# An output projection in twelve rounded products in a token-mixing and mixture-of-experts kernel

## The reference, cut to what matters

```python
x_prev = concatenate([zeros_like(x[:, :1]), x[:, :-1]], axis=1)
xk, xv, xr = (x_prev + (x - x_prev) * tm for tm in (tmk, tmv, tmr))
k, v, r = xk @ Wk.T + bk, xv @ Wv.T + bv, xr @ Wr.T + br
wkv = _wkv_scan(k, v, time_decay, time_first)   # a recurrence over time
out = (sigmoid(r) * wkv) @ Wo.T + bo            # the output projection
x1 = layernorm(x + out)
# each token goes to the best of 8 experts: probs = softmax(x1 @ wg)
y = layernorm(x1 + gate * (x1 @ W[expert].T + b[expert]))
```

## Time and profile before

| | |
|---|---|
| median of 3 runs | 608.55 us (607.44 to 608.61) |
| the profiled execution | 608.08 us, span 606.4 us |
| TensorE busy | 566.6 us (93%) |
| VectorE busy | 530.0 us (87%) |
| ScalarE busy | 436.2 us (72%) |
| GpSimd busy | 281.4 us (46%) |
| mean granted clock of TensorE | 0.978 of full speed |

### The profile page before, as it was taken

The page is one execution under the profiler, slowest core; times in us unless marked ns, Lnnn a source line. Parts: engine busy times, 40 slices in busy tenths (PEclk is TensorE's granted clock), DMA queues, the critical chain, the costliest instruction groups (busy, mean ns, idle before and its releaser), DMA issues. The chain is left out here.

```text
span 606.4 us, 8730 instructions
## 1 busy us (share of the span) xinstructions
PE 566.6 (93%) x2404; PEld 408.3 (67%) x2404; DVE 530.0 (87%) x815; ACT 436.2 (72%) x838; POOL 281.4 (46%) x221
## 2 busy tenths in 40 slices
PE   4997689999999999999999999999989999999990
PEld 1444466677677768767776866885557888788880
DVE  6889989998998999899899989899999698766760
ACT  3637656677587667758766775956975998899982
POOL 2768515544452553445355344531051565666631
PEclk9999799999999999999999999999997999999996
DMA  9352550094046109305701920767854696878840
GB/s 348 138 70 81 203 66 0 1 248 101 0 174 139 36 14 247 85 0 187 141 17 39 251 57 1 221 138 265 256 162 134 184 255 205 266 228 224 237 150 0
DMA packets 40984, 84.46 MB, mean 139 GB/s; under 512 B 8751, under 2 KB 8751, under 8 KB 40818
## 3 DMA queue, kind: packets, MB, share of 16 engines
q1 hardware_dynamic: 30482, 56.67, 28.4%
q0 software_dynamic: 10464, 27.33, 20.9%
HBM read 66.95 MB, written 35.65 MB: 169 GB/s over the span
## 5 line engine op out<-in xcount | busy, mean ns | idle before, releaser
L1168 POOL TENSOR_TENSOR mixed<-unsplit,mixed 128x1024 fp32r<-128x1024 f32 x42 | 100.0, 2402 | 117.9 <-ACT mixed L775 117.9
L705 PE MATMUL y_ps<-w_e_hi,xgT 128*128 x312 | 108.8, 410 | 0.4 <-issue 0.4
L539 PE MATMUL y_ps<-w_o,rw 128*128 128x512 f32 x224 | 100.8, 594 | 0.0
L526 PE MATMUL vb<-mixed,w_kvr 128*128 128x512 f32 x336 | 87.8, 411 | 6.9 <-DVE evn L1375 6.8
L526 PE MATMUL kb<-mixed,w_kvr 128*128 128x512 f32 x336 | 82.4, 394 | 5.7 <-POOL mixed L1168 3.1
L526 PE MATMUL rb<-mixed,w_kvr 128*128 128x512 f32 x336 | 86.8, 407 | 0.9 <-DVE ee L1389 0.9
L526 PEld LDWEIGHTS vb<-mixed,w_kvr 128*128 128x128 f32 x336 | 63.4, 193 | 24.9 <-DVE evn L1375 8.9
L526 PEld LDWEIGHTS kb<-mixed,w_kvr 128*128 128x128 f32 x336 | 62.1, 188 | 21.6 <-DVE state L1343 5.2
L526 PEld LDWEIGHTS rb<-mixed,w_kvr 128*128 128x128 f32 x336 | 62.5, 188 | 19.5 <-issue 5.7
L1184 POOL TENSOR_TENSOR ee<-ee,state 128x512 f32<-128x512 f32 x32 | 35.0, 1092 | 86.8 <-DVE state L1359 86.1
L1326 DVE SCALAR_TENSOR_TENSOR unsplit<-diff,vec,xb 128x512 f32<-128x512 f32 x96 | 68.2, 772 | 5.3 <-PE kb L526 5.0
(11 more groups left out here) (233 smaller groups left out, 1105.7 us busy)
## 6 DMA issues: line engine op xcount, KB each, us to landing
bias<-b_experts SPq DMA_DIRECT2D x39, 256.0 KB, 4.6
x_biased<-bo POOLq DMA_DIRECT2D x8, 1024.0 KB, 17.4
w_e_raw<-w_experts SPq DMA_DIRECT2D x8, 1024.0 KB, 7.9
rows<-x_biased SPq DMA_DIRECT2D x28, 256.0 KB, 3.5
x_rows<-rows SPq DMA_DIRECT2D x28, 256.0 KB, 6.7
xb<-xT SPq DMA_DIRECT2D x4, 1026.0 KB, 5.4
xb<-xT SPq DMA_DIRECT2D x3, 1024.0 KB, 5.1
w_raw<-w_square SPq DMA_DIRECT2D x2, 1024.0 KB, 10.4
```

The costliest lines, as they stand in the source:

```text
L526: mm = pe.matmul(bank, w_kvr[m][:, a, h, o:o + P], mixed[m][:, bb, h, :], start=(k == 0), stop=(k == 3 * CH - 1))
L539: mm = pe.matmul(y_ps[:, j % 2, :], rw[:, half, c, j * P:(j + 1) * P], w_o[:, c, :], start=(c == 0), stop=(c == CH - 1))
L705: mm = pe.matmul(y_ps[:, n % 2, :], xgT[n % 3][:, a, c, :], w[:, bass.ds(p, 1), c, :].rearrange("p u o -> p (u o)"), start=(c == 0 and (a, ...
L1168: pool.tensor_tensor(mixed[m][:, LO, 2 * hp:2 * hp + 2, :], unsplit[m][:, LO, 2 * hp:2 * hp + 2, :], mixed[m][:, HI, 2 * hp:2 * hp + 2, :] ...
```

## The change

The output projection uses rounded parts, as the other products do. `result` writes the raw product over `er`; ScalarE's new `result_hi` rounds it (two copies of 128x512 for each pair), VectorE's new `result_lo` subtracts (two of 128x512 for each pair), and `out_pair` forms the twelve products of a tile. `w_o` is split once, in block 1, by ScalarE and GpSimd (`out_weight_lo`, two of 128x1024). In blocks 0 to 6 the averages and shifts go from VectorE to ScalarE's `deviation`. `er` and the parts get places of their own (`even`, `odd`, `late`, `end`), with waits that guard them. Expert `e` lies at place `e`: `home`, `moved_e` and `slot_...` go, and the loads of the experts and their rounding stand at other points. The last block's output tiles 0 and 1 are formed in two halves. GpSimd scatters a tile one step later.

```diff
-        rw_at = base + 6 * mat
-        rw = place("rw", [P, HALVES, CH, TB], F32, at=rw_at)
...
+        w_o_raw = place("w_o_raw", [P, CH, H], F32, at=w_o_lo_at)
+        w_o_lo = place("w_o_lo", [P, CH, H], F32R, at=w_o_lo_at)
...
+        w_o = place("w_o", [P, CH, H], F32R)
...
-        er = place("er", [P, 2, 2, TB], F32)
...
+        part_places = {"even": (even_at, even_at + 4 * TB, even_at + pair), "odd": (odd_at, odd_at + 4 * TB, odd_at + pair),
+                       "late": (pad_at + pair, spare_at, pad_at)}
+        rw_hi, rw_lo, er = {}, {}, {}
+        for name, (hi0_at, hi1_at, lo_at) in part_places.items():
+            rw_hi[name] = [place(f"rw_hi_{name}{c}", [P, TB], F32R, at=at) for c, at in enumerate((hi0_at, hi1_at))]
+            rw_lo[name] = place(f"rw_lo_{name}", [P, 2, TB], F32R, at=lo_at)
+            er[name] = place(f"er_{name}", [P, 2, TB], F32, at=lo_at)
+        er["end"] = place("er_end", [P, 2, TB], F32, at=temps_at)
...
+        guess_in = {(0, 0): "even", (0, 1): "late", (1, 0): "odd", (1, 1): "late", (END, 0): "odd", (END, 1): "end"}
+        parts_in = {**guess_in, (END, 1): "even"}
...
-                    sp.wait_ge(r_filled, CH)
-                    sp.wait_ge(w_lo[R], PAIRS)
-                    sp.dma_start(w_o[:], w_v[O]).then_inc(w_loaded[O], 16)
+                    sp.dma_start(w_o_raw[:], w_v[O]).then_inc(w_loaded[O], 16)
...
-            load_experts((0, 1))
+            load_experts((6,))
...
             sp.wait_ge(k_filled, CHUNKS)
-            load_experts((2, 3))
+            load_experts((0, 1))
             sp.wait_ge(v_filled, CHUNKS)
-            load_experts((4, 5))
+            load_experts((2, 3, 4, 5))
...
-            load_experts((6, 7))
+            sp.wait_ge(y_filled, last * TPB)
+            load_experts((7,))
             store_rows(last - 1, range(TPB))
...
+            def out_pair(bank, half, p, j):
+                name = parts_in[half, p]
+                for c in range(2 * p, 2 * p + 2):
+                    hi = rw_hi[name][c % 2][:, j * P:(j + 1) * P]
+                    lo = rw_lo[name][:, c % 2, j * P:(j + 1) * P]
+                    pe.matmul(bank, hi, w_o[:, c, :], start=(c == 0), stop=False)
+                    pe.matmul(bank, hi, w_o_lo[:, c, :], start=False, stop=False)
+                    mm = pe.matmul(bank, lo, w_o[:, c, :], start=False, stop=(c == CH - 1))
+                return mm
             def project_out(n, half, j):
-                pe.wait_ge(wkv_done, n * 2 + 2)
+                pe.wait_ge(wkv_done, n * CH + CH)
                 pe.wait_ge(y_taken, n * TPB + (j + 1))
                 if isinstance(n, int) and n == 0 and j == 0:
-                    pe.wait_ge(w_loaded[O], 16)
+                    pe.wait_ge(wo_lo, PAIRS)
                     pe.wait_ge(route_const, 1)
-                for c in range(CH):
-                    mm = pe.matmul(y_ps[:, j % 2, :], rw[:, half, c, j * P:(j + 1) * P], w_o[:, c, :],
-                                   start=(c == 0), stop=(c == CH - 1))
-                mm.then_inc(y_filled, 1)
+                out_pair(y_ps[:, j % 2, :], half, 0, j)
+                out_pair(y_ps[:, j % 2, :], half, 1, j).then_inc(y_filled, 1)
...
+            def out_first(j):
+                pe.wait_ge(wkv_done, last * CH + 2)
                 if j == 0:
                     pe.wait_ge(den_ready, CHUNKS)
-                elif j == 1:
+                else:
                     pe.wait_ge(evn_ready, CHUNKS)
-                else:
-                    pe.wait_ge(y_taken, last * TPB + (j - 1))
-                for c in range(CH):
-                    mm = pe.matmul(bank, rw[:, HALVES - 1, c, j * P:(j + 1) * P], w_o[:, c, :], start=(c == 0), stop=(c == CH - 1))
-                mm.then_inc(y_filled, 1)
+                out_pair(last_banks[j], END, 0, j)
+            def out_second(j):
+                pe.wait_ge(wkv_done, CHUNKS)
+                out_pair(last_banks[j], END, 1, j).then_inc(y_filled, 1)
...
+            def out_last(j):
+                pe.wait_ge(wkv_done, CHUNKS)
+                pe.wait_ge(y_taken, last * TPB + (j - 1))
+                out_pair(last_banks[j], END, 0, j)
+                out_pair(last_banks[j], END, 1, j).then_inc(y_filled, 1)
...
-            out_last(0)
+            out_first(0)
+            out_first(1)
+            out_second(0)
             turn_rows(before, 0)
-            out_last(1)
+            out_second(1)
...
-            def reciprocal_guess(i, p):
+            def reciprocal_guess(i, half, p):
                 g = i * 2 + p
+                er_p = er[guess_in[half, p]]
+                if (half, p) == (END, 1):
+                    act.wait_ge(newton, i * 2 + 1)
+                elif not isinstance(i, int) or i + p > 1:
+                    act.wait_ge(y_filled, (i + p - 1) * TPB)
                 act.wait_ge(den_ready, i * CH + (2 * p + 2))
...
+            def result_hi(i, half, p):
+                act.wait_ge(rw_raw, i * 2 + (p + 1))
+                if (half, p) == (END, 1):
+                    act.wait_ge(y_filled, last * TPB)
+                for c in range(2):
+                    act.activation(rw_hi[parts_in[half, p]][c][:], er[guess_in[half, p]][:, c], ACT.Copy).then_inc(rw_rounded, 1)
...
             def deviation(n, h):
                 two = slice(2 * h, 2 * h + 2)
+                act.wait_ge(y_taken, n * TPB + (2 * h + 4))
+                act.activation(mean[:, two], row_sum[:, two], ACT.Copy, scale=-1.0 / H).then_inc(stats_done, 2)
+                wait(act, logits_done, n * TPB)
                 act.wait_ge(stats_done, n * TPB + (2 * h + 2))
-                wait(act, logits_done, n * TPB)
...
+                act.wait_ge(rstd_ready, n * 2 + (h + 1))
+                act.activation(nmr[:, 2 * h:2 * h + 1], mean[:, 2 * h:2 * h + 1], ACT.Copy, scale=rstd[:, 2 * h:2 * h + 1])
+                act.activation(nmr[:, 2 * h + 1:2 * h + 2], mean[:, 2 * h + 1:2 * h + 2], ACT.Copy,
+                               scale=rstd[:, 2 * h + 1:2 * h + 2]).then_inc(nmr_ready, 1)
...
                 enter_ab(i, 1, *here)
+                if s.prev:
+                    result_hi(m, 1 - s.half, 1)
+                if s.prev and not s.prev2:
+                    act.wait_ge(w_loaded[O], 16)
+                    act.wait_ge(r_filled, CH)
+                    act.wait_ge(w_lo[R], PAIRS)
+                    act.activation(w_o[:], w_o_raw[:], ACT.Copy).then_inc(wo_hi, 1)
...
                 enter_ab(i, 3, *here)
+                result_hi(i, s.half, 0)
                 mix_hi(i + 1, V, 0)
...
-            reciprocal_guess(before, 1)
+            reciprocal_guess(before, 0, 1)
             deviation(earlier, 1)
...
             enter_ab(last, 1, *here)
+            result_hi(before, 0, 1)
             move_turned(earlier, 2)
...
-            act.wait_ge(k_filled, CHUNKS)
-            expert_hi(0)
-            reciprocal_guess(last, 0)
+            reciprocal_guess(last, END, 0)
             entry_weight(last, 3)
             gate_r(last, 2)
             decay(last, 3)
             weight(last, 3)
             enter_ab(last, 3, *here)
+            result_hi(last, END, 0)
+            act.wait_ge(k_filled, CHUNKS)
+            expert_hi(0)
+            gate_r(last, 3)
+            reciprocal_guess(last, END, 1)
             expert_hi(1)
-            gate_r(last, 3)
-            reciprocal_guess(last, 1)
             act.wait_ge(a_scanned, CHUNKS)
             deviation_before(0)
+            result_hi(last, END, 1)
...
+            act.wait_ge(y_filled, TILES)
             move_gathered(0, 0)
             move_gathered(1, 1)
-            act.wait_ge(y_filled, TILES)
+            expert_hi(6)
             expert_hi(7)
...
+            def out_weight_lo(hp):
+                half = slice(2 * hp, 2 * hp + 2)
+                pool.wait_ge(wo_hi, 1)
+                pool.tensor_tensor(w_o_lo[:, half], w_o_raw[:, half], w_o[:, half].bitcast(F32), ALU.subtract).then_inc(wo_lo, 1)
...
                 leave(i, 1)
+                if not s.prev2:
+                    for hp in range(PAIRS):
+                        out_weight_lo(hp)
...
-                scatter(k)
+                if k > 0:
+                    scatter(k - 1)
+            scatter(SORTED - 1)
...
                 if c % 2 == 0 and not (isinstance(i, int) and i == 0):
-                    dve.wait_ge(wkv_done, i * 2 + (c // 2 - 1))
+                    dve.wait_ge(rw_raw, i * 2 + (c // 2 - 1))
...
-                if not isinstance(i, int) or i > 1:
-                    dve.wait_ge(y_filled, (i - 1) * TPB)
                 dve.wait_ge(num_added, i * CH + (2 * p + 2))
-                dve.scalar_tensor_tensor(out=rw[:, half, 2 * p:2 * p + 2, :], in0=evn[:, p], scalar=-1.0,
-                                         in1=er[:, p], op0=ALU.mult, op1=ALU.mult).then_inc(wkv_done, 1)
+                dve.scalar_tensor_tensor(out=er_p[:], in0=evn[:, p], scalar=-1.0,
```

(41 more changed lines are left out.)

106 lines of the change are left out of this document (54 added, 52 removed).

## The result

The changed kernel takes 622.56 us (median of 4 runs, 620.3 to 623.91), the kernel before in the same comparison 608.03: the ratio is 1.0235, 95% interval 1.0201 to 1.0269. The sign of the forecast was right; the size, +14.5 us instead of +4, lies outside its range. The profiled execution, the slowest of the four, took 623.91 us; its span is 621.9, and its mean granted clock is 0.955 (0.978 before). One run of act_order, a kernel further down, took 2333.54 us and is left out of its median and ratio.

What follows compares the result with a forecast made beforehand. TensorE was taken to bound the middle blocks narrowly, VectorE close behind, and the expert stage; -3.0 (middle blocks) + 2.7 (second block) + 4.0 (last block) = +3.7 us on 608.55 gave 612.2 us, range 605.6 to 615.5.

Steps and rivals of the forecast that it cites:

- the cover in the middle block's last item: Middle blocks: ScalarE's waits for TensorE cover its added roundings, averages and shifts, so its exponent of rb(0) is in time.
- The sum: Whole kernel: -3.0 middle blocks, +2.7 second block, +4.0 last block, together +3.7 us.
- forecast 3.0: Five middle blocks: -0.6 us each, -3.0 in all, as removed averages and waits outweigh added remainders.
- forecast 2.05: Last block up to the wait for the logits: +2.05 us, from recurrence 1 starting 2.15 late.
- Block 1: Second block, once: VectorE's remainders meet GpSimd's w_o remainders, +4.6, less 1.9 returned: +2.7 us; -1.6 without any meeting.
- The single meeting: Rival, second block: the weights' remainders meet VectorE only once, for one half of 2.4 us; 609.8 us, chance 0.21.
- The last block's lag: Last block: ScalarE has the exponent ready 13.0 us after ev, so recurrence 1 starts 2.15 us late.
- Two bare pairs: Last block's last half: two remainder pairs uncovered, +2.45 us, less 0.5 for three small routing operations that go.
- VectorE's own work as the period: First rival, middle and last blocks: ScalarE keeps up, blocks are 50.7 us, change is faster; 605.7 us, chance 0.24.
- The clock rival: Second block: TensorE waits 4.8 us for evn, its clock falls and following products cost double; 615.1 us, chance 0.15.
- Twelve products: Output tiles on TensorE: twelve rounded products cost 2.72 instead of 3.44 us, freeing 2.9 a block, no term of the sum.
- The expert stage: Stage from 458.5 us on: TensorE bounds it, its length stays and only its start can move; 0.

Runs made afterwards that it cites:

- act_order: Changed kernel with only ScalarE's order changed: copy of turned tile 1 before rounding the second result pair, shifts in the norm, one last-block norm later; 620.85 us.
- filler: Changed kernel plus never-read TensorE products where it waits for x1T: six per middle block, twelve in the last block; 613.73 us, ratio 1.0079.
- experts_late: Changed kernel with rounding and remainders of experts 6 and 7 moved behind the second expert tile; 623.46 us, ratio 1.0252.
- wo_window: Changed kernel with w_o's rounding and remainders one chunk sooner, GpSimd first waiting for VectorE's last reciprocal result; 616.13 us, ratio 1.0120.
- combined: Changed kernel with act_order's middle part, wo_window, odd_later and TensorE's last-block products ahead of the logits; 612.56 us, ratio 1.0056.
- odd_later: Changed kernel with the last half's first remainder pair behind VectorE's next row sum and gate cap; 617.31 us, ratio 1.0142.
- fill_b1: filler plus 18 more never-read products in block 1, where TensorE waits for evn ahead of vb(3); 614.88 us, ratio 1.0106.
- stats_on_dve: Changed kernel with averages and shifts back on VectorE, nothing else; 622.38 us, ratio 1.0233.
- norm_late: filler without its twelve last-block products, with another last-block order on ScalarE and TensorE instead; 615.49 us, ratio 1.0135.
- combined2: combined with norm_late's last-block order, and block 1's chunk 1 additions ahead of GpSimd's output bias transfer; 609.48 us, ratio 1.0011.
- no_remainders: Changed kernel with VectorE's result remainders cut to one column, the third product reading the rounded part again; 614.82 us, ratio 1.0106.

## Why the prediction was wrong

- **The step that failed** is the cover in the middle block's last item, "it waits for TensorE 0.99 us ahead of the exponent at 338.64 and several us for each distance". I asked only when ScalarE's exponent of `rb` is due at VectorE. ScalarE also feeds TensorE, with the copies `x1T`, and TensorE waits for them in its own order ahead of everything else. In the changed kernel it does so 9 times from 124 to 381 us, 9.4 us, and before it never did. The sum put this at nothing. The waits alone do cost little (blocks without a fall took 51.6 to 52.0 us, and 51.3 to 51.6 with shorter waits in act_order); the clock that falls behind them costs some 1.7 us in a middle block and 1.6 to 2.9 in the last. I took the clock to fall behind VectorE's lag in block 1, not here.
- **With the clock held up the sum was nearly right.** filler's middle blocks are 2.8 us under before (forecast 3.0), the first three steps of its last block 2.6 over (forecast 2.05), and its ratio makes +4.8 us of the forecast +3.7. I missed 10.8 us; by the two ratios filler returns 9.5. Of these, 4.0 lie in the middle blocks: that is the granted clock behind the waits for `x1T`, shown by the 35 blocks and by filler. The last block's 2.9 are the clock too, as `rb(0)` at 4.76 and 3.01 us shows; that the fill brought them back is less sure, since experts_late had them without it (no fall in the two kernels with the fill there, five in the six without). The rest lies in stages whose code is the same (the experts 2.85, with the wait for `x1T_last`), and is those executions' scatter.
- **Block 1**, +2.7, measured +3.3 and +2.5 in other executions of the same code; wo_window, at 52.22 against 52.54 before, shows that all of it is the meeting with `w_o_lo`, though without the meeting I had put the block 1.6 us under before and it was only 0.3. Right in mechanism, and near in size. The single meeting didn't happen: the pair was held for both halves.
- **The last block's lag**, +2.15 by an exponent at 13.0 us after `ev`: with the clock up, the cap stands 13.5 us after it in filler and 13.7 in combined, and the last block's three steps are 2.6 us longer than before. Nearly right; the other 2.9 us of the changed kernel's profiled execution are the clock.
- **Two bare pairs, +2.45 less 0.5**, measured +3.46. The term was mis-sized by the meeting at 430.85 (1.0 us, shown by odd_later), and by the 0.5: the small routing operations that go stand behind `ids_full` in VectorE's queue (`moved_e` at 445.78 before, `ids_full` at 444.83), so this stage can't return them.
- **VectorE's own work as the period**, the first rival: not reached, though its sign was there. The exponent of `rb(0)` came in time in every middle block, but VectorE waits for later ones, at two caps a block (ten times, 5.4 us). Blocks without a fall are 51.3 to 52.0 us, not 50.7, and VectorE's work in remainders is worth 0.4 us there.
- **The clock rival** had the right mechanism in the wrong place, at a chance of 0.15. The fall in block 1 costs nothing (fill_b1).
- **Twelve products** at 2.8 us: right. TensorE's 2.9 us a block turned into 0.9 at best (act_order), and in the changed kernel into less than nothing.
- **The expert stage** unchanged: not contradicted, within a scatter of 3.7 us. The scatters' and loads' new order was not tried by itself.

Still open: which execution gets a fall and which doesn't. The same code took 17.80, 16.44 and 14.87 us for the last block's first step, and stats_on_dve had a wait of 1.80 us at the same place with no fall behind it. The runs without a profile show the same: of norm_late's six, four took 614.9 to 615.6 us at a mean granted clock of 0.969 to 0.972, and two took 620.4 and 620.9 at 0.958. The Trainium skill, page "TensorE: Matmul & The Clock Gate", section "Part 1: The HAM clock gate", says of a kernel's start that the same kernel shows different numbers of products at the lower rate from run to run; here the same holds in the middle of a kernel, by the three steps above. A single profile therefore prices a fall only within some 3 us.

## What to carry to other kernels

When work moves to an engine with idle time, look up everything that engine produces and who takes it, not only the result that the bounding engine takes: here the dearest consumer was an in-order queue with a row of due work behind a small wait. Ask for each new wait of TensorE what the next product is for: at half rate it costs if its result was nearly due (1.5 to 3 us here) and nothing if it had time. Place a two-input subtraction of GpSimd beside VectorE's instructions that read PSUM, and where it lies beside two-input ones, count it on VectorE too (here 3.9 us of VectorE for 4.7 of GpSimd). Before a single profile is believed, look for the same stretch of code in other executions: here seven of them showed what one could not.

## What the runs showed of the hardware

- Waits of TensorE of only 1.55 and 1.59 us (changed kernel at 191.44, combined2 at 392.23) were followed by twelve products at 4.45 and 4.47 us. Twelve take 3.0 at 2.4 GHz and 5.2 to 5.5 at 1.2 GHz (and 99.04 above), so most of them ran at the lower level. It is not every time: behind the same wait of 1.55 us at 245.01 in the changed kernel they took 3.01, and in 21 of 35 such places there was no fall. With products that nobody reads ahead of the logits there was no fall in 15 such places (filler, fill_b1, norm_late).
- A VectorE subtraction of one column waited as long as one of 512 for GpSimd's running subtraction: the first of the two at 84.56 in no_remainders took 1.89 us, the second 0.15; the first of 512 columns, at 85.53 in the changed kernel, took 2.43, where `rw_lo_even` takes 0.70 in the mean.
